# Attention: two PSUM rooms for turned scores and one for plain scores, and both key halves of the values in one slot

## The reference, cut to what matters

```python
xn = layernorm(x)                                  # x: (8, 256, 256)
q, k, v = rope(xn @ Wq + bq), rope(xn @ Wk + bk), xn @ Wv + bv   # 16 heads of 16
scores = einsum("bshd,bthd->bhst", q, k) / 4;  scores = where(causal, -inf, scores)
out = einsum("bhst,bthd->bshd", softmax(scores), v) @ Wo + bo
y = x + out + moe(xn)      # 64 experts, top 6 of them, and 2 shared experts
```

## Time and profile before

| | us |
|---|---|
| median of 3 runs (660.39 to 664.65) | 662.77 |
| the profiled execution | 666.26 |
| its span | 664.4 |
| fill and first eight slots, 502.00 to 531.09 | 29.09 |
| one batch of eight slots, 567.31 to 585.41 | 18.10 |
| from the last plain score's slot to the end, 635.24 to 664.40 | 29.16 |

### The profile page before, as it was taken

How to read it: one execution, slowest core, us unless ns; L and a number is a source line. 1 busy time by engine, 2 the same in 40 slices (tenths; PEclk the granted TensorE clock), 3 DMA queues, 4 the chain that set the end, 5 groups by cost and what they waited for, 6 DMA issues and landing times.

```text
span 664.4 us, 17821 instructions
## 1 busy us (share of the span) xinstructions
PE 625.2 (94%) x4928; PEld 368.9 (56%) x4929; DVE 437.2 (66%) x1328; ACT 308.0 (46%) x798; POOL 360.4 (54%) x376
## 2 busy tenths in 40 slices
PE   6999999988989999899999989999999999999997
PEld 3644455654455555555555555555554666666654
DVE  6768678456474766656566575654446688898864
ACT  3653121033343444444444444454445767777752
POOL 3000000278685877868787686874300766666662
PEclk9999999999899999999999999999999999999999
DMA  8600011238869789796887969987425777777432
GB/s 272 189 32 1 0 34 33 94 95 269 264 183 264 243 250 286 211 325 200 261 281 228 307 198 298 286 251 163 98 58 190 213 217 228 221 219 222 130 103 74
DMA packets 78167, 124.52 MB, mean 187 GB/s; under 512 B 11113, under 2 KB 52618, under 8 KB 78090
## 3 DMA queue, kind: packets, MB, share of 16 engines
q1 hardware_dynamic: 43098, 60.18, 29.4%
q0 software_dynamic: 15872, 46.16, 24.5%
q10 hardware_dynamic: 19120, 17.18, 7.7%
HBM read 85.73 MB, written 37.75 MB: 186 GB/s over the span
## 4 chain that ended last, share of the span: by engine, by line
PE 78%; DVE 5%; issue 4%; ACT 4%; POOL 3%; DMA 3%; ACTq 2%; SPq 0%; DVEq 0%; POOLq 0%
PE pair L1181 22%; PE pair L1208 15%; PE pair L1151 6%; PE pair L1138 4%; PE pair L1086 4%; PE bank L1293 4%; PE bank L1192 3%; PE bank L1165 3%; PE bank L1325 2%; PE pair L1048 2%; DVE negm L950 2%; ACTq L616 2%; PE pair L1248 2%; PE pair L1267 1%; PE bank L1304 1%
## 5 line engine op out<-in xcount | busy, mean ns | idle before, releaser
L453 POOL DMA_INDIRECT lower<-xn_rows,idx_all x128 | 134.0, 1047 | 194.8 <-DVE idx_all L925 107.2
L1181 PE MATMUL pair<-space,work 128*64 (+1 forms) x768 | 167.3, 466 | 12.0 <-ACT work L601 7.6
L1208 PE MATMUL pair<-lower,work 88*64 x512 | 123.1, 380 | 5.2 <-ACT lower L614 2.7
L1181 PEld LDWEIGHTS pair<-space,work 128*64 128x64 f32 x768 | 67.4, 138 | 84.6 <-issue 63.4
L869 DVE TENSOR_TENSOR work<-work,pair 128x176 f32<-128x176 f32 x128 | 42.5, 337 | 105.2 <-ACT work L608 104.4
L1208 PEld LDWEIGHTS pair<-lower,work 88*64 88x64 f32 x512 | 68.7, 136 | 55.5 <-issue 22.6
L1181 PE MATMUL pair<-wqkv_sb,work 128*64 128x352 f32 x256 | 90.6, 477 | 0.0
L614 ACT ACTIVATE lower<-pair 128x256 f32<-128x256 f32 x128 | 49.2, 384 | 79.7 <-PE pair L1208 79.7
L518 POOL DMA_INDIRECT wqkv_sb<-y_rows,slot_i x48 | 47.2, 984 | 60.9 <-DVE negm L950 34.0
L601 ACT ACTIVATE work<-pair 128x256 f32<-128x256 f32 x128 | 42.4, 381 | 69.0 <-PE pair L1138 39.9
L950 DVE TENSOR_REDUCE negm<-pair 128x2 f32<-128x256 f32 (+1 forms) x128 | 64.9, 551 | 11.4 <-PE pair L1256 10.2
(11 more groups left out here) (198 smaller groups left out, 1199.8 us busy)
## 6 DMA issues: line engine op xcount, KB each, us to landing
space<-wgu SPq DMA_DIRECT2D x66, 352.0 KB
y_rows<-lower ACTq DMA_DIRECT2D x128, 128.0 KB, 4.0
qk_all<-qk_rows SPq DMA_DIRECT2D x64, 256.0 KB, 4.2
lower<-wdn SPq DMA_DIRECT2D x64, 176.0 KB
qk_rows<-qk_all POOLq DMA_DIRECT2D x32, 256.0 KB
qk_rows<-space POOLq DMA_DIRECT2D x16, 256.0 KB
xn_rows<-qk_all SPq DMA_DIRECT2D x16, 128.0 KB, 2.0
lower<-xn_rows,idx_all POOLq DMA_INDIRECT x128
```

The lines of the kernel that those rows point to most:

```text
L453: po.indirect_dma_start(xg[:, r % XB, :], None, xn_rows[:, :], bass.IndirectOffsetOnAxis(idx_all[:, r:r + 1], 0)).then_inc(xg_in[r % XB], 16)
L1181: last = pe.matmul(pair[u % 2][strip, 0:2 * F], xgT[u][:, c, strip], n, start=c == 0, stop=c == EC - 1, skip_group_check=True)
L1208: last = pe.matmul(pair[u % 2][strip, 512:512 + E], hT[:, u % 2, c, strip], n, start=c == 0, stop=c == 1, skip_group_check=True)
```

## The change

Plain scores now use `pair[0]` alone, and turned scores alternate between `pair[1]` and `pair[2]`. The first nine plain scores, which run before any turned score, use all three rooms in turn. The waits follow: from m = 10 on `score_masks(m)` waits for the maxima of pair m-1, and `turned_masks(n)` for the exponentials of pair n-2. Both key halves of the values stand in the even slot. No instruction is added or removed, and no size changes.

```diff
-        score_room = [pair[0], pair[2]]
+        def score_room(m):
+            return pair[m % 3] if m < AHEAD else pair[0]
+        def turned_room(n):
+            return pair[1 + n % 2]
...
             def score_masks(m):
-                if m >= 2:
-                    pe.wait_ge(max_ok, m - 1)
+                if m >= 3:
+                    pe.wait_ge(max_ok, m - 2 if m <= AHEAD else m)
...
             def turned_masks(n):
-                if n:
-                    pe.wait_ge(exp_done, n)
+                if n >= 2:
+                    pe.wait_ge(exp_done, n - 1)
+                else:
+                    pe.wait_ge(max_ok, AHEAD - 1 + n)
...
                 if NS <= n < NS + 6:
-                    keep_on(bank[0][:], DRAIN[n - NS])
+                    keep_on(pair[0][:, 0:512], DRAIN[n - NS])
                 if n % 2 == 0 and 0 <= w < QUADS:
                     values(w, 0)
-                if n % 2 == 1 and 0 <= (n - 3) // 2 < QUADS:
-                    values((n - 3) // 2, 1)
+                    values(w, 1)
```

More of the change, by code:

```diff
@@ L658, in exps @@
                     act.wait_ge(av_ok, (n - G) // 2 + 1)
-                act.activation(pT[:, n % G], pair[1][:].rearrange("p (j k) -> p j k", j=2)[:, :, 0:SPAN],
+                act.activation(pT[:, n % G], turned_room(n)[:].rearrange("p (j k) -> p j k", j=2)[:, :, 0:SPAN],
                                ACT.Exp).then_inc(exp_done, 1)
@@ L944, in maxes @@
             def maxes(m):
-                scores = score_room[m % 2][:].rearrange("p (j k) -> p j k", j=2)
+                scores = score_room(m)[:].rearrange("p (j k) -> p j k", j=2)
                 dve.wait_ge(s_ok, m + 1)
@@ L1242, in score_masks @@
             def score_masks(m):
-                if m >= 2:
-                    pe.wait_ge(max_ok, m - 1)
+                if m >= 3:
+                    pe.wait_ge(max_ok, m - 2 if m <= AHEAD else m)
                 for h in range(2):
                     for j in range(2):
-                        o = score_room[m % 2][:, 512 * j:512 * (j + 1)].rearrange("p (s k) -> p s k", s=2)[:, :, 0:P]
+                        o = score_room(m)[:, 512 * j:512 * (j + 1)].rearrange("p (s k) -> p s k", s=2)[:, :, 0:P]
                         pe.matmul(o, id_b[own[j], h], mask_b[own[j], h].unsqueeze(1).to_broadcast([64, 2, P]),
@@ L1255, in scores @@
                     for j in range(2):
-                        last = pe.matmul(score_room[m % 2][:, 512 * j + qt * P:512 * j + (2 * qt + 1) * P],
+                        last = pe.matmul(score_room(m)[:, 512 * j + qt * P:512 * j + (2 * qt + 1) * P],
                                          q[own[j], qt * P:(qt + 1) * P], k[own[j], 0:(qt + 1) * P],
@@ L1261, in turned_masks @@
             def turned_masks(n):
-                if n:
-                    pe.wait_ge(exp_done, n)
+                if n >= 2:
+                    pe.wait_ge(exp_done, n - 1)
+                else:
+                    pe.wait_ge(max_ok, AHEAD - 1 + n)
                 for h in range(2):
                     for j in range(2):
-                        o = pair[1][:, 512 * j:512 * (j + 1)].rearrange("p (s k) -> p s k", s=2)[:, :, 0:P]
+                        o = turned_room(n)[:, 512 * j:512 * (j + 1)].rearrange("p (s k) -> p s k", s=2)[:, :, 0:P]
                         pe.matmul(o, mask_b[own[j], h], id_b[own[j], h].unsqueeze(1).to_broadcast([64, 2, P]),
@@ L1274, in turned_scores @@
                 for j in range(2):
-                    pe.matmul(pair[1][:, 512 * j:512 * j + SPAN], pick[own[j], x], mT[own[j], b % 2],
+                    pe.matmul(turned_room(n)[:, 512 * j:512 * j + SPAN], pick[own[j], x], mT[own[j], b % 2],
                               start=False, stop=False, skip_group_check=True)
@@ L1278, in turned_scores @@
                     for j in range(2):
-                        last = pe.matmul(pair[1][:, 512 * j + 2 * P * kb:512 * j + S + P * kb],
+                        last = pe.matmul(turned_room(n)[:, 512 * j + 2 * P * kb:512 * j + S + P * kb],
                                          k[own[j], kb * P:(kb + 1) * P], q[own[j], kb * P:S],
```

## The result

| | before | after |
|---|---|---|
| median, us (20 runs each, same chip) | 662.7 | 664.84 (662.52 to 668.67) |
| ratio, with its interval | | 1.0036 [1.0019, 1.0053] |
| the same two measured again (22 and 12 runs) | 663.71 | 664.53, ratio 1.0007 [0.9982, 1.0032] |
| the profiled execution: span | 664.4 | 661.2 |
| in it, attention: first plain masks to the end of the span | 161.27 | 162.24 |

The forecast was 668.6, +0.9%. The time is inside the range on record, and attention is longer, as forecast, but by +1.0 us where +5.8 was forecast. Between no change and 0.5% slower is what the two measurements leave. (The ratios and intervals are as on record; they are not quotients of the medians. One of the 22 runs, 672.98 us at a mean granted clock of 0.949, is slow and not counted in them.)

A forecast was written before the change was run, and what follows sets the result against it. PE was taken as the bound, still for only 0.85 us of an 18.10 us batch. Terms -0.8 + 0.7 + 4.9 + 0.5 + 0.5 = +5.8 us gave 668.6 us against the median, +0.9%, range 663.5 to 674.

The forecast's parts named there:

- walked: Slot-by-slot reckoning of one attention batch from the old trace's durations: 19.08 us in place of 18.10, +0.98.
- The added wait: One plain room makes PE's next plain masks wait for DVE's maxima; no slot can be shorter than 1.75 us.
- The removed wait: Turned scores waiting for exponentials, 5.7 us over attention; removing it gives nothing in steady slots, no gain at the end.
- The values' second half: Moved from odd to even slot at 0.36 us; PE's even slot becomes 2.45, the odd 1.15 plus its extra.
- The sum is ... 17.25: PE's work in one batch counted from group start to start, 17.25 us, leaving PE still for only 0.85 of 18.10.
- Fill: Plain scores ahead of slot 0: three rooms let PE run ahead and DVE's waits between maxima go, -0.8 us.
- first eight slots: Attention's first eight slots, where slots 0 to 3 have no `combine`: 17.15 us against 16.46, +0.7.
- five batches: Five whole batches from slot 8, each 0.98 us longer: +4.9 us.
- six slots: The six slots behind the five whole batches: 14.14 us against 13.63, +0.5.
- end: End of attention: second key half ahead of `back` costs 0.36, later last `normalise` 0.15; +0.5 us, between 0 and 0.9.
- rival 2: Both waits hide, DVE's lateness in slots 6 and 7 absorbed elsewhere: -1 to +2, 662 to 665 us; 12%.
- rival 3: In even slots `normalise` pushes DVE's next maxima past a 0.12 margin; at 0.3 excess 6.9 us more, 675; 13%.

The follow-up runs named there:

- rooms only: The changed kernel with the values' second key half put back in the odd slot, new rooms kept; ratio to the kernel before 0.9992 [0.9968, 1.0016].
- merge only: The kernel before with its old rooms, only both key halves of the values put into the even slot; ratio to it 1.0005 [0.9985, 1.0025].

## Why the prediction was off

By its own steps, slot by slot (n%8) of one batch, forecast against after:

| | 0 | 1 | 2 | 3 | 4 | 5 | 6 | 7 | batch |
|---|---|---|---|---|---|---|---|---|---|
| walked | 2.45 | 1.75 | 2.56 | 1.75 | 2.56 | 3.07 | 2.45 | 2.49 | 19.08 |
| measured | 2.30 | 1.75 | 2.42 | 1.74 | 2.42 | 3.07 | 2.30 | 2.51 | 18.51 |

- **The added wait: right.** Loop of 1.75, stops behind slots 1 and 7, none elsewhere; from start to start they have the sizes walked, 0.60 and 0.70. DVE's reductions start 0.67 behind the masks and hold the next masks for 1.08, as read from the fill.
- **The removed wait: right.** It gave nothing in a steady slot. Slots 1 and 2, where the turned scores had to wait, take 3.95 together with either set of rooms while the halves are apart (before, rooms only), and 4.16 and 4.17 with the halves merged (merge only, after).
- **The values' second half: the term that was mis-sized.** "PE's work per slot becomes 0.46 + 0.69 + 0.57 + 0.36 + 0.37 = 2.45 (even)": the 0.36 was the price of the half where it stood alone in the odd slot, and was moved unchanged. Behind the first half it costs 0.79 - 0.57 = 0.22. That is 0.14 in each of the four even slots, and no other slot differs by more than 0.02: 19.08 - 4 x 0.14 = 18.52, against 18.51 measured. "The sum is ... 17.25" was therefore no floor for the changed kernel; it is 17.25 - 0.56 = 16.69, and PE stands still for 1.82 of a batch, where 1.83 was forecast. The batch with `back` between the halves, 18.92, shows it from the other side. It stays 0.16 under the walk's 19.08 because its `back` starts 0.57 behind the values in place of the walk's 0.93, and in slots 6 and 7 DVE, not `back`, then sets the end.
- **The sum.** Fill -1.0 (forecast -0.8), first eight slots +0.04 (+0.7), five batches +2.0 (+4.9), six slots +0.07 (+0.5), end -0.15 (+0.5): +1.0. The forecast lies 4.8 too high. The 32 groups of values, at 0.14 each, come to 4.5 of it, by stretch: first eight slots 0.4 (3 groups) of 0.66, five batches 2.8 (20) of 2.9, six slots 0.4 (3) of 0.43, end 0.8 (6) of 0.65; the fill adds 0.2. For the batches this is measured. For the other stretches it is a count that fits roughly: slot 7 of the first eight is also 0.2 shorter than walked, and in the end PE stops for `raw_copy` too, so that the run with `back` between the halves is only 0.5 longer there than after.
- **The rivals.** The time is the one of rival 2, but not by its mechanism: the waits did not hide. `normalise` did not push the maxima in slots 2 and 4 (rival 3); slots 1, 3 and 5 have the lengths walked, 1.75, 1.74 and 3.07. A shorter even slot brings `back` forward by as much as it brings the next masks forward.

**What stays open:** attention explains +1.0 us, 0.15%. The first measurement says 0.19 to 0.53%, the second -0.18 to 0.32%. A run's mean granted clock, which in the profiles falls ahead of attention, goes with its time: of after's 20 runs the nine with a mean granted clock of 0.999 or more have a median of 663.25, the eleven at 0.997 or less one of 666.19. In the second measurement the clocks of both kernels' runs are on record, and those at 0.999 or more give 663.39 (7 runs) against 662.30 (12), +1.1, about what attention explains. For before's 20 runs of the first measurement they are not on record, so whether its 0.36% holds more than attention's part stays open.

## What to carry to other kernels

A group's price read from start to start holds the passage to the group behind it; when an edit puts two like groups back to back, work out the sum both with the old prices and with one passage less, and keep both in the range. When rooms are shared out between two consumers, the one that gets a single room sets a loop (here 1.75 us, plain scores on DVE; or 0.44 of stop, turned scores on ACT): look for independent work to put into that stop before taking the room back. A term that lies ahead of the changed stage in the trace is no part of the comparison: measure the stage from its own start.

## What the runs showed of the hardware

The passage, from the values' weights of 32 columns to the 128 columns of the group behind them, is seen in PE's weight loads. In before, with the halves apart (start, length, loads; idle ahead in brackets):

```profile
568.45 0.16 PEld L1293 LDWEIGHTS bank<-pT,v_all 128*32 128x32 f32 x8
569.02 0.20 PEld L1304 LDWEIGHTS bank<-id_f,raw 128*128 128x128 f32 x2 [0.41 <-issue]
...
570.54 0.16 PEld L1293 LDWEIGHTS bank<-pT,v_all 128*32 128x32 f32 x8
570.89 0.11 PEld L1248 LDWEIGHTS pair<-rope_sb,id_b 64*128 64x128 bf16 x4 [0.20 <-issue]
```

and in after, with the halves together:

```profile
568.25 0.62 PEld L1300 LDWEIGHTS bank<-pT,v_all 128*32 128x32 f32 x16 [0.17 <-issue]
569.07 0.20 PEld L1311 LDWEIGHTS bank<-id_f,raw 128*128 128x128 f32 x2 [0.20 <-issue]
```

With `back` between the halves both pauses are there again:

```profile
567.50 0.20 PEld L1311 LDWEIGHTS bank<-id_f,raw 128*128 128x128 f32 x2 [0.41 <-issue]
567.87 0.16 PEld L1300 LDWEIGHTS bank<-pT,v_all 128*32 128x32 f32 x8 [0.17 <-issue]
568.23 0.11 PEld L1253 LDWEIGHTS pair<-rope_sb,id_b 64*128 64x128 bf16 x4 [0.20 <-issue]
```

In these rows the weights behind a run of 32-column loads come late, by 0.41 behind the half that moves 256 columns and 0.20 behind the half that moves 128; with the halves together only the 0.20 is left. From start to start 0.14 is saved for each passage that goes. How the pause of 0.41 turns into 0.14 of PE's time is not shown by these rows. Nor is it shown whether the width of the weights makes the price, or any change of group would: no run changes the passages between other groups alone.
